# A recurrent layer with experts and grouped attention: the gate's sign products, the last group's end and the reciprocals, reordered

## The chip, the cores and the metric

The kernel runs on 1 core of a Trainium2 chip. The metric is the device time of one execution in microseconds; the number to compare is the median over the runs. The engines are named PE (TensorE, matmul), DVE (VectorE), ACT (ScalarE), POOL (GpSimd) and SP (SyncE, which only issues transfers here). PSUM has eight banks of 128 x 512 fp32, `bank[0]` to `bank[7]`.

## What is computed

Two layers over 2 x 512 tokens of 256 channels. Layer 0 is a chunked selective scan gated by a mixture of 8 experts; it ends at about 315 us and is not touched here. Layer 1, cut to what matters:

```python
q = rope((xn @ Wq.T).reshape(2, 512, 32, 64)); k = rope((xn @ Wk.T).reshape(2, 512, 8, 64)); v = ...
logits = where(causal, q @ k.T / 8, min)          # 4 query heads share one of 8 k/v heads
s = softmax(logits) @ v @ Wo.T
a = sign(layernorm(x) * gamma + beta); signed_w = sign(weight - mean(weight, 1))
g = silu((a @ signed_w.T + bias) * alpha)
x = x + s * g
```

## The kernel before

**Groups and steps.** The 8 k/v heads are 8 groups, worked one after the other. A group has 4 pairs of query heads, a pair 5 steps: 20 steps of one score bank each, some 2.4 us long. `schedule(kind)` (line 76) writes out, as a list of (step, priority, operation, index, index), what happens in each step; every engine walks the same sorted list in `attend` and does its own share of each entry. Within a step the smaller priority comes first. Work that runs over a group's end is "late" and is done in the next group's steps. The kinds are one "first", six "middle", one "last" group, and then "tail", which has only the late work of the last one and the list `ends`.

**The operations** (i is the pair, k the step within it; "b" a batch, "m" a half of the channels):

- **S**: PE computes a bank of scores (L1793 to L1796); DVE takes the negated row maximum (L1031, L1035) into `nmax`.
- **E**: ACT exponentiates the bank with the maximum as bias into `prob`, and accumulates the row sums (L1279).
- **N**, twice a pair, at steps 5i+3 and 5i+5: DVE takes the reciprocal of a head's four row sums (L1040), and POOL multiplies the head's four blocks of `prob` by it (L1471: 128, 256, 384 and 512 columns). DVE first waits on `exp_done` for the exponentials of the step before.
- **T**, 6 steps behind S: PE transposes a bank of `prob` (L1509), ACT copies it rounded to `p_hi` (L1286), DVE subtracts to get `p_lo` (L1044, one input in PSUM). T with k = 0 and k = 2 waits for POOL's products of the pair's first and second head.
- **A**, 2 steps behind T: three products with V on PE (L1513 to L1515). **O** turns a finished pair into `o_hi` (ACT L1293) and `o_lo` (DVE L1048).
- **W**: PE multiplies by Wo for one batch and one half of the channels, DVE adds to `sT` (L1056).
- **Vh, Vl**: the next V rounded to `v_hi` (ACT L1317), and `v_lo` = V - `v_hi` (DVE L1013, both inputs in SBUF, 128 x 256). In the middle and last groups Vl stands in steps 3 and 13, behind N.
- **Q, r, a, h, l**: the next queries: product (PE), rope into `q_mix` (DVE L1001, L1002, one input in PSUM), add (POOL L1480), `q_hi` (ACT L1257), `q_lo` (POOL L1483). **VQ, VO, Kh, Kl**: the same splitting for Wq (POOL L1451), Wo (ACT L1297, POOL L1475) and K (ACT L1264, POOL L1455).
- **Z**: one of the four sign products of the gate (PE L1850, bank 0 or 1), and its Silu on ACT into `g1T` (L1329).

**Order around N.** On every engine an instruction starts only when those ahead of it in its own queue have. On DVE the order within a step is O, S, T, N, Vl, W, r; on POOL N, then a, l, Kl. VO comes ahead of all others of its step, which is step 14; POOL's order there is the four products of step 13, then `wo_lo`, then those of step 15.

**The end.** Before the tail PE waits for the last exponentials (`exp_done`), since Z uses banks 0 and 1. In the tail Z0 to Z3 stand behind A(3,1), A(3,3), A(3,4) and W2. After the list, DVE waits for all W and all four Silus, does the four products `sT * g1T` (L1098), PE transposes them back (L1509, 16 transposes into banks 0 to 3), DVE adds the four banks to `x_tok` (L1102), and SP sends out each half of `x_tok` (L646) when it is complete.

Of the kernel before, what the change touches and what calls it, by code (L numbers as in the profile page):

```python
# [11 lines left out]
P = 128  # L12
BATCH, SEQ, C = 2, 512, 256
T = BATCH * SEQ
NT = T // P
TB = SEQ // P
# [56 lines left out]
def schedule(kind):  # L73

    own = [(14, 0, "VO", 0, 0), (1, 8, "Kh", 1, 0), (2, 6, "Kl", 1, 0)]
    for r in range(PAIRS):
        for k in range(5):
            n = 5 * r + k
            own += [(n, 2, "S", r, k), (n, 4, "E", r, k), (n + LAG, 3, "T", r, k), (n + LAG + TO_V, 5, "A", r, k)]
        for h in range(2):  # L80
            own += [(5 * r + HEADS_AT[h], 5, "N", r, h)]
        own += [(5 * r + 4 + LAG + TO_V + 1, 1, "O", r, 0)]
# [21 lines left out]
    else:  # L104
        ready += [(0, 1, "VQ", 0, 0)] + half(2, 3, 0) + half(3, 13, 0)
    ends = [(4 + 2 * n, 8.6, "Z", n, 0) for n in range(KC * BATCH)]
    lists = {"first": [(own, False), (ready, False)], "middle": [(own, True), (own, False), (ready, False)],
# [56 lines left out]
def layered_kernel(nc, x, params, consts, select, rope, w_in, w_out, w_moe, w_moe_tail, w_qkv, w_o, w_sign, out):  # L164
# [4 lines left out]
    with ctx:  # L169
# [301 lines left out]
        def _(sp):  # L471
# [170 lines left out]
            move_q(KVH - 1, 1)  # L642
            for b in range(BATCH):
                sp.wait_ge(x_ready, NT // 2 + (b + 1) * TB // 2)
                ts = slice(b * TB, (b + 1) * TB)
                sp.dma_start(out.rearrange("(t p) c -> p t c", p=P)[:, ts, :], x_tok[:, ts, :]).then_inc(out_done, 16)  # L646
            sp.wait_ge(out_done, BATCH * 16)


        @block.vector  # L650
        def _(dve):
# [369 lines left out]
            def attend(now, steps):  # L1021
                for late, op, i, k in steps:
# [26 lines left out]
                    elif op == "W":  # L1049
# [3 lines left out]
                        if g == 0:  # L1053
                            vec.tensor_copy(sT[:, m, cs], bank[6 + m][:, :]).then_inc(w_added[m], 1)
                        else:
                            TT(sT[:, m, cs], sT[:, m, cs], bank[6 + m][:, :], ALU.add).then_inc(w_added[m], 1)  # L1056
                    elif op == "r":
                        rope_q(now * 2 + i, k)
# [32 lines left out]
            attend(KVH, schedule("tail"))  # L1091
            for m in range(KC):
                dve.wait_ge(w_added[m], KVH * BATCH)
            for n in range(KC * BATCH):
                s, m = n // KC, n % KC
                cs = slice(s * HALF, (s + 1) * HALF)
                dve.wait_ge(g1_ready, KC * BATCH)
                TT(sT[:, m, cs], sT[:, m, cs], g1T[:, m, cs], ALU.mult).then_inc(sg_ready, 1)  # L1098
            for n in range(NT // 2):
                dve.wait_ge(back_full, n + 1)  # L1100
                xt2 = x_tok[:, 2 * n:2 * n + 2, :]
                TT(xt2, xt2, bank[n][:, :].rearrange("p (t c) -> p t c", c=C), ALU.add).then_inc(x_ready, 1)  # L1102


        @block.scalar
        def _(act):
# [159 lines left out]
            def attend(now, steps):  # L1266
                for late, op, i, k in steps:
# [58 lines left out]
                    elif op == "Z":  # L1326
                        m, s = i // 2, i % 2
                        act.wait_ge(sign_full, i + 1)
# [178 lines left out]
        def _(pe):  # L1507
# [263 lines left out]
            def attend(now, steps, held):  # L1771

                for late, op, i, k in steps:
# [68 lines left out]
                    elif op == "G":  # L1842
                        turn_norm(i, h_ready, bank[6 + i % 2])
                        held[i % 2] = (sign_ready, i + 1)
                    elif op == "Z":
                        m, s = i // 2, i % 2
                        if i > 1:
# [41 lines left out]
            attend(KVH, schedule("tail"), [(w_added[m], (KVH - 1) * BATCH) for m in range(KC)])  # L1889
            for n in range(NT // 2):  # L1890
                pe.wait_ge(sg_ready, KC * (n // (TB // 2) + 1))
                for j in range(2 * KC):
                    t, m = 2 * n + j // KC, j % KC
                    ins = tr(bank[n][:, j * P:(j + 1) * P], sT[:, m, t * P:(t + 1) * P])
                ins.then_inc(back_full, 1)

# [72 lines left out]
```

## Time and profile before

| | us |
|---|---|
| median of 3 runs (767.24 to 769.56) | 767.31 |
| profiled execution: time | 765.41 |
| profiled execution: span | 763.6 |
| PE busy | 712.9 (93%) |
| PE weight load busy | 623.1 (82%) |
| DVE busy | 482.1 (63%) |
| ACT busy | 416.7 (55%) |
| POOL busy | 397.5 (52%) |
| mean granted PE clock | 0.986 |

The profile is of one execution; its span lies inside its time, and the 1.8 us between the two are around the program. Times in the rows are counted from the span's start. The attention groups run from about 336 to 735 us, one group in 48.9 us in the steady part, and the tail from there to 763.6. A row's "idle before" counts from the recorded end of the engine's preceding instruction.

### The profile page before, as it was taken

What the parts mean: (1) busy time and instruction counts of PE and PEld (TensorE: products, weight loads), DVE (VectorE), ACT (ScalarE), POOL (GpSimd) and SP (SyncE); (2) the same over time, 40 slices, a digit from 0 to 9 for tenths busy, and PEclk for the clock granted to TensorE, in tenths of its full rate; (3) what the DMA queues carried; (4) which work ended last, traced back from release to release, by engine and by line L of the source; (5) the groups of instructions that cost most, each with busy time, mean ns of one, the idle gap of its engine ahead of it and who ended that gap; (6) DMA issues with size and microseconds to landing.
All of it is one profiled execution on the core that took longest, in us unless ns stands there. A gap on an engine that the chain in (4) does not pass through costs nothing.

```text
span 763.6 us, 13451 instructions
## 1 busy us (share of the span) xinstructions
PE 712.9 (93%) x4576; PEld 623.1 (82%) x4576; DVE 482.1 (63%) x1030; ACT 416.7 (55%) x1043; POOL 397.5 (52%) x449
## 2 busy tenths in 40 slices
PE   2999999999999999796979999999999999999995
PEld 2887989989989897575768888888888888888883
DVE  7582655334333427866557777777787777777764
ACT  4446244134243233466466677667766777667662
POOL 1412442422332322138487787677867778677460
PEclk9999999999999999899899999999999999999999
DMA  8186877776877835173133322232223322132001
GB/s 292 37 259 191 280 247 233 244 250 191 279 238 239 246 86 138 32 226 84 56 106 82 77 66 60 70 90 64 63 68 78 90 54 66 48 91 57 1 1 56
DMA packets 103828, 98.06 MB, mean 128 GB/s; under 512 B 50576, under 2 KB 74064, under 8 KB 103632
## 3 DMA queue, kind: packets, MB, share of 16 engines
q1 hardware_dynamic: 101648, 91.43, 41.3%
q0 software_dynamic: 2112, 5.77, 2.3%
q8 instruction: 37, 0.61, 0.3%
q14 instruction: 31, 0.25, 0.1%
HBM read 69.24 MB, written 11.14 MB: 105 GB/s over the span
## 4 chain that ended last, share of the span: by engine, by line
PE 64%; DVE 11%; POOL 10%; ACT 7%; issue 4%; SPq 2%; DMA 1%; DVEq 0%; ACTq 0%
PE bank L1653 14%; PE bank L1687 8%; PE bank L1509 7%; PE bank L1513 7%; PE bank L1514 7%; PE bank L1515 7%; POOL prob L1471 5%; ACT prob L1279 3%; PE bank L1793 3%; DVE nmax L1035 2%; PE bank L1794 2%; POOL q_lo L1483 2%; ACT p_hi L1286 2%; DVE o_lo L1048 1%; POOL wq_lo L1451 1%
## 5 line engine op out<-in xcount | busy, mean ns | idle before, releaser
L1471 POOL TENSOR_TENSOR prob<-prob,rinv 128x128 f32<-128x128 f32 (+3 forms) x256 | 177.6, 725 | 103.0 <-DVE rinv L1040 103.0
L1279 ACT ACTIVATE prob<-bank,nmax 128x512 f32<-128x512 f32 (+3 forms) x256 | 133.2, 528 | 48.0 <-DVE nmax L1035 47.7
L1044 DVE TENSOR_TENSOR p_lo<-bank,p_hi 128x512 fp32r<-128x512 f32 x160 | 110.1, 688 | 52.5 <-ACT p_hi L1286 51.6
L1286 ACT ACTIVATE p_hi<-bank 128x512 fp32r<-128x512 f32 x160 | 96.3, 602 | 76.9 <-PE bank L1509 76.8
L1653 PEld LDWEIGHTS bank<-xgT,wm 128*128 128x128 f32 x920 | 108.7, 192 | 4.5 <-issue 2.9
L1653 PE MATMUL bank<-xgT,wm 128*128 128x128 f32 x920 | 111.3, 275 | 0.5 <-ACT xgT L1195 0.5
L1035 DVE TENSOR_REDUCE nmax<-bank 128x1 f32<-128x512 f32 (+2 forms) x192 | 91.2, 503 | 16.3 <-PE bank L1796 15.8
L1509 PE MATMUL bank<-cst,prob 128*128 128x128 f32 x640 | 97.9, 276 | 3.0 <-ACT prob L1279 1.2
L1793 PE MATMUL bank<-kT,qT 128*128 128x512 f32 (+3 forms) x256 | 82.2, 326 | 12.4 <-ACT prob L1279 6.9
L1513 PE MATMUL bank<-p_hi,v_lo 128*128 128x128 f32 (+3 forms) x256 | 92.9, 363 | 0.3 <-DVE p_lo L1044 0.3
L1442 POOL DMA_INDIRECT y_rows<-y_row,to_row x21 | 22.7, 1081 | 118.3 <-DVE y_row L904 92.6
L1515 PE MATMUL bank<-p_hi,v_hi 128*128 128x128 f32 (+3 forms) x256 | 82.3, 322 | 0.0
L1514 PE MATMUL bank<-p_lo,v_hi 128*128 128x128 f32 (+3 forms) x256 | 82.3, 322 | 0.0
L1509 PEld LDWEIGHTS bank<-cst,prob 128*128 128x128 f32 x640 | 73.7, 142 | 6.0 <-POOL prob L1471 3.3
L1794 PE MATMUL bank<-kT,qT 128*128 128x512 f32 (+3 forms) x256 | 74.7, 323 | 0.0
L1793 PEld LDWEIGHTS bank<-kT,qT 128*128 128x128 f32 x256 | 48.4, 189 | 22.5 <-issue 8.4
L1220 ACT ACTIVATE sil<-bank 128x512 f32<-128x512 f32 x23 | 13.7, 597 | 75.9 <-PE bank L1653 75.9
L1687 PE MATMUL bank<-wm,hE 128*128 128x256 f32 x230 | 53.5, 379 | 1.2 <-DVE y_low L909 1.2
L1279 ACT ACTIVATION_READ_ACCUMULATOR prob<-bank,nmax 128x1 f32 x256 | 52.4, 205 | 0.0
L944 DVE TENSOR_TENSOR hE<-sil,bank 128x512 f32<-128x512 f32 x23 | 15.8, 688 | 57.5 <-PE bank L1653 40.6
L1794 PEld LDWEIGHTS bank<-kT,qT 128*128 128x128 f32 x256 | 48.6, 190 | 3.9
L1515 PEld LDWEIGHTS bank<-p_hi,v_hi 128*128 128x128 f32 x256 | 48.4, 189 | 2.7
(307 smaller groups left out, 1534.8 us busy)
## 6 DMA issues: line engine op xcount, KB each, us to landing
wm<-in_w_moe SPq DMA_DIRECT2D x23, 1280.0 KB, 5.8
wm<-in_w_moe SPq DMA_DIRECT2D x23, 640.0 KB, 5.1
qT<-q_hi SPq DMA_DIRECT2D x124, 64.0 KB, 2.0
qT<-q_lo SPq DMA_DIRECT2D x124, 64.0 KB, 2.0
k_exp<-k_rows SPq DMA_DIRECT2D x56, 64.0 KB, 2.0
wtl<-in_w_moe_tail SPq DMA_DIRECT2D x46, 64.0 KB, 5.4
y_rows<-gate SPq DMA_DIRECT2D x1, 2048.0 KB, 13.7
wq_raw<-in_w_qkv SPq DMA_DIRECT2D x32, 64.0 KB, 2.5
```

Source lines behind the costliest of these rows:

```text
L1044: TT(p_lo[:, b_, :], bank[2 + b_ % 2][:, :], p_hi[:, b_, :].bitcast(F32), ALU.subtract).then_inc(plo_done, 1)
L1279: ins = actv(prob[:, i % 2, h, POFF[j]:POFF[j] + (j + 1) * P], bk[:, at:at + (j + 1) * P], ACT.Exp, bias=nmax[:, i % 2, h, j:j + 1], accum ...
L1286: actv(p_hi[:, b_, :], bank[2 + b_ % 2][:, :], ACT.Copy).then_inc(phi_done, 1)
L1471: ins = GT(seg, seg, rinv[:, i % 2, k, j:j + 1].to_broadcast([P, (j + 1) * P]), ALU.mult)
L1509: return nc.tensor.transpose(dst, src, ident)
L1513: mm(dst, w_l, m_h, start=start, stop=False)
L1514: mm(dst, w_h, m_l, start=False, stop=False)
L1515: return mm(dst, w_h, m_h, start=False, stop=stop)
L1653: ins = mm(dst, w(c), xgT[:, u, c, :], start=c == 0, stop=c == KC - 1)
L1687: ins = mm(bank[3][:, 0:C], hE[:, u, i * P:(i + 1) * P], wm[:, s, i, PJ:WM] if i < FULL else ptl[:, s, :], start=i == 0, stop=i == HC - 1)
L1793: mm(dst, qs, kT[:, b, 0, 0:n], start=(h, j, at) == SCORES[k][0], stop=False)
L1794: mm(dst, qs, kT[:, b, 1, 0:n], start=False, stop=False)
```

## The change

Three things are done:

- **N** gets priority 2.6 in place of 5 in all groups. On DVE the reciprocal then stands behind S and ahead of T; Vl, which stood directly behind N, stands behind T.
- In the tail, **Z** n stands in step n: behind the first steps' W, T, A in place of behind the last ones. Z0 and Z1 now make batch 0's gate, Z2 and Z3 batch 1's.
- The closing products, transposes and additions become operations of the tail's list: **M** (DVE product `sT * g1T` for one half of the channels and one batch), **B** (PE, two transposes back), **X** (DVE addition to `x_tok` of one bank). Those of batch 0 stand among the last steps: M(0,0) behind T(3,3), M(1,0) behind T(3,4), B0 ahead of A(3,4), B1 behind it, X0 and X1 behind O3. Those of batch 1 stand behind W2 and W3. The output is sent in three pieces: batch 0, then a quarter, then the last quarter.

```diff
@@ schedule
         for h in range(2):
-            own += [(5 * r + HEADS_AT[h], 5, "N", r, h)]
+            own += [(5 * r + HEADS_AT[h], 2.6, "N", r, h)]
...
-    ends = [(4 + 2 * n, 8.6, "Z", n, 0) for n in range(KC * BATCH)]
+    ends = [(n, 8.6, "Z", n, 0) for n in range(KC * BATCH)]
+    ends += [(4 + m, 9, "M", m, 0) for m in range(KC)] + [(10 + m, 9, "M", m, 1) for m in range(KC)]
+    ends += [(6 + n, 9, "B", n, m) for n in range(2) for m in range(KC)] + [(11 + m, 9.1, "B", n, m) for m in range(KC) for n in (2, 3)]
+    ends += [(8 + n, 9.2, "X", n, 0) for n in range(2)] + [(13, 9.2, "X", n, 0) for n in (2, 3)]
@@ SP
-            for b in range(BATCH):
-                sp.wait_ge(x_ready, NT // 2 + (b + 1) * TB // 2)
-                ts = slice(b * TB, (b + 1) * TB)
+            for lo, hi in ((0, TB), (TB, TB + 2), (TB + 2, NT)):
+                sp.wait_ge(x_ready, NT // 2 + hi // 2)
+                ts = slice(lo, hi)
                 sp.dma_start(out.rearrange("(t p) c -> p t c", p=P)[:, ts, :], x_tok[:, ts, :]).then_inc(out_done, 16)
@@ DVE, attend
+                    elif op == "M":
+                        cs = slice(k * HALF, (k + 1) * HALF)
+                        dve.wait_ge(w_added[i], (KVH - 1) * BATCH + (k + 1))
+                        dve.wait_ge(g1_ready, KC * (k + 1))
+                        TT(sT[:, i, cs], sT[:, i, cs], g1T[:, i, cs], ALU.mult).then_inc(sg_ready, 1)
+                    elif op == "X":
+                        dve.wait_ge(back_full, i + 1)
+                        xt2 = x_tok[:, 2 * i:2 * i + 2, :]
+                        TT(xt2, xt2, bank[i][:, :].rearrange("p (t c) -> p t c", c=C), ALU.add).then_inc(x_ready, 1)
@@ DVE, behind the tail
-            for m in range(KC):
-                dve.wait_ge(w_added[m], KVH * BATCH)
-            for n in range(KC * BATCH):
-                s, m = n // KC, n % KC
-                cs = slice(s * HALF, (s + 1) * HALF)
-                dve.wait_ge(g1_ready, KC * BATCH)
-                TT(sT[:, m, cs], sT[:, m, cs], g1T[:, m, cs], ALU.mult).then_inc(sg_ready, 1)
-            for n in range(NT // 2):
-                dve.wait_ge(back_full, n + 1)
-                xt2 = x_tok[:, 2 * n:2 * n + 2, :]
-                TT(xt2, xt2, bank[n][:, :].rearrange("p (t c) -> p t c", c=C), ALU.add).then_inc(x_ready, 1)
@@ ACT and PE, attend
                     elif op == "Z":
-                        m, s = i // 2, i % 2
+                        m, s = i % 2, i // 2
@@ PE, attend
+                    elif op == "B":
+                        b = i // 2
+                        pe.wait_ge(sg_ready, KC * b + k + 1)
+                        if i < 2:
+                            pe.wait_ge(g1_ready, KC * BATCH)
+                        for t in range(2):
+                            ins = tr(bank[i][:, (t * KC + k) * P:(t * KC + k + 1) * P],
+                                     sT[:, k, (2 * i + t) * P:(2 * i + t + 1) * P])
+                        if k == KC - 1:
+                            ins.then_inc(back_full, 1)
@@ PE, behind the tail
-            for n in range(NT // 2):
-                pe.wait_ge(sg_ready, KC * (n // (TB // 2) + 1))
-                for j in range(2 * KC):
-                    t, m = 2 * n + j // KC, j % KC
-                    ins = tr(bank[n][:, j * P:(j + 1) * P], sT[:, m, t * P:(t + 1) * P])
-                ins.then_inc(back_full, 1)
```

## Rows read from the trace of the kernel before

**Rows 1.** Totals of waits, 330 to 764 us: total us, times, longest.

```profile
POOL prob L1471 <- DVE rinv L1040: 103.0, 48, 6.6
...
PEld bank L1509 <- POOL prob L1471: 3.3, 10, 1.4
```

**Rows 2.** Chain of waits, 632 to 652 us: start, us, what.

```profile
641.39 0.09 DVE rinv L1040
...
641.55 2.76 POOL prob L1471 x4
...
650.81 0.66 PE bank L1509 x4
```

**Rows 3.** Timeline around step 3, group 2: start, us, engine, line, operation [idle before <-releaser].

```profile
458.19 0.17 DVE L1040 RECIPROCAL rinv<-rsum 128x4 f32<-128x4 f32 x1
458.28 0.39 DVE L1013 TENSOR_TENSOR v_lo<-v_exp,v_hi 128x256 fp32r<-128x256 f32 x1
...
458.44 2.84 POOL L1471 TENSOR_TENSOR prob<-prob,rinv 128x128 f32<-128x128 f32 x4 [1.90 <-DVE rinv L1040]
...
458.74 0.76 DVE L1035 TENSOR_REDUCE nmax<-bank 128x1 f32<-128x384 f32 x2
...
459.81 0.69 DVE L1044 TENSOR_TENSOR p_lo<-bank,p_hi 128x512 fp32r<-128x512 f32 x1 [0.31 <-ACT p_hi L1286]
...
461.93 0.69 DVE L1035 TENSOR_REDUCE nmax<-bank 128x1 f32<-128x512 f32 x1 [0.24 <-PE bank L1796]
...
463.01 0.69 DVE L1044 TENSOR_TENSOR p_lo<-bank,p_hi 128x512 fp32r<-128x512 f32 x1 [0.38 <-ACT p_hi L1286]
```

**Rows 4.** Timeline around step 13, group 1.

```profile
434.14 2.85 POOL L1471 TENSOR_TENSOR prob<-prob,rinv 128x128 f32<-128x128 f32 x4 [3.14 <-DVE rinv L1040]
...
434.29 0.75 DVE L1035 TENSOR_REDUCE nmax<-bank 128x1 f32<-128x384 f32 x2
...
435.24 0.69 DVE L1044 TENSOR_TENSOR p_lo<-bank,p_hi 128x512 fp32r<-128x512 f32 x1 [0.20 <-ACT p_hi L1286]
...
436.95 1.28 POOL L1475 TENSOR_TENSOR wo_lo<-wo_raw,wo_hi 128x512 fp32r<-128x512 f32 x1
```

**Rows 5.** Timeline, last group: a score's weight load.

```profile
704.77 0.19 PEld L1793 LDWEIGHTS bank<-kT,qT 128*128 128x128 f32 x1 [0.39 <-ACT prob L1279]
```

**Rows 6.** Timeline, layer 0: a POOL and a DVE product, both on SBUF tiles.

```profile
112.94 1.05 POOL L1398 TENSOR_TENSOR decay_in<-cst,dts 128x512 f32<-128x512 f32 x1
112.97 1.57 DVE L877 TENSOR_TENSOR state<-state,since 128x512 f32<-128x512 f32 x1 [0.92 <-PE bank L1621]
```

**Rows 7.** Timeline, first group, a v_lo of step 7.

```profile
354.05 2.53 POOL L1483 TENSOR_TENSOR q_lo<-q_mix,q_hi 128x512 fp32r<-128x512 f32 x2
...
356.08 2.03 DVE L1013 TENSOR_TENSOR v_lo<-v_all,v_hi 128x256 fp32r<-128x256 f32 x1
...
356.53 1.30 POOL L1460 TENSOR_TENSOR v_all<-v_all 128x512 f32<-128x512 f32 x1
```

**Rows 8.** Timeline of the tail.

```profile
736.02 0.66 PE L1509 MATMUL bank<-cst,prob 128*128 128x128 f32 x4 [1.19 <-ACT prob L1279]
...
744.84 0.60 PE L1850 MATMUL bank<-signT,wsT 128*128 128x512 bf16 x2
...
748.18 0.19 PEld L1513 LDWEIGHTS bank<-p_hi,v_lo 128*128 128x128 f32 x1 [0.83 <-DVE p_lo L1044]
...
750.66 0.47 PE L1513 MATMUL bank<-o_hi,wo_lo 128*128 128x512 f32 x1 [1.05 <-DVE o_lo L1048]
...
752.33 0.69 DVE L1056 TENSOR_TENSOR sT<-sT,bank 128x512 f32<-128x512 f32 x1 [1.82 <-PE bank L1515]
...
754.96 2.50 DVE L1098 TENSOR_TENSOR sT<-sT,xnT 128x512 f32<-128x512 f32 x4
...
757.37 2.47 DVE L1102 TENSOR_TENSOR x_tok<-x_tok,bank 128x512 f32<-128x512 f32 x4
```

**Rows 9.** Transfers, 750 to 764 us: GB/s in 40 slices of 0.35 us.

```profile
GB/s 0 0 0 0 0 47 0 0 0 0 0 0 0 0 0 0 0 0 0 0 0 0 0 0 0 0 0 170 351 345 307 366 337 354 345 345 76 0 0 0
```

More of the change, by code:

```diff
@@ L642, in _ @@
             move_q(KVH - 1, 1)
-            for b in range(BATCH):
-                sp.wait_ge(x_ready, NT // 2 + (b + 1) * TB // 2)
-                ts = slice(b * TB, (b + 1) * TB)
+            for lo, hi in ((0, TB), (TB, TB + 2), (TB + 2, NT)):
+                sp.wait_ge(x_ready, NT // 2 + hi // 2)
+                ts = slice(lo, hi)
                 sp.dma_start(out.rearrange("(t p) c -> p t c", p=P)[:, ts, :], x_tok[:, ts, :]).then_inc(out_done, 16)
-            sp.wait_ge(out_done, BATCH * 16)
+            sp.wait_ge(out_done, 3 * 16)
         @block.vector
@@ L1844, in attend @@
                         held[i % 2] = (sign_ready, i + 1)
+                    elif op == "B":
[8 more added lines that the diff above has]
+                            ins.then_inc(back_full, 1)
                     elif op == "Z":
-                        m, s = i // 2, i % 2
+                        m, s = i % 2, i // 2
                         if i > 1:
```

## The prediction

> **What bounds the kernel now.** The page's shares come first: TensorE works 93% of the span, so in each stage the question is who holds TensorE up. Then the totals of waits from 330 us on: GpSimd sits 103 us idle before the products, waiting for reciprocals, yet TensorE in turn waited for products only 3.3 us, in ten places, 1.4 of it in one [rows 1]. GpSimd's idle time as such is worth nothing; those places are. The chain of waits of a middle group shows one: reciprocal at 641.39, then products, q_lo, wq_lo, the next products, and only then TensorE at 650.81 [rows 2]. GpSimd works through these jobs without a pause, so the start of the first sets the end of the last. Last comes the tail, from 736 us to the end, read as a timeline [rows 8].
>
> **Part 1a, N before T: what it gives.** The vector engine's order S, T, N becomes S, N, T (letters as in the section on the kernel). Its instructions of 0.69 start 0.60 apart, so the N at 458.19 moves to 457.60, and GpSimd starts at 457.84 in place of 458.44 [rows 3]. Does N now wait? It needs the exponentials of the step before. For the 62 reciprocals that have a T ahead I set the end of those exponentials beside the end of S: all but one are done by then (closest 0.06 us); the one is the tail's, which still comes 2.1 us earlier than now. So TensorE's waits for GpSimd go. The 1.4 is a place without a T ahead and stays; the other nine average 0.21 [rows 1], and with the overlap between instructions that each breaks I take 0.26 at the six middle places like 650.81 and 0.2 at two of the last group: 2.0 us. Where T itself waited for p_hi, N falls into that gap and leaves a vector chain on which TensorE later waits: 0.08 apiece, 12 times, 1.0. Together 3.0; bounds 0 (the wait only passes to another engine) and 3.6.
>
> **Part 1b: what it costs.** In steps 3 and 13 of every group but the first, Vl follows. Before: N 458.19, v_lo 458.28, products 458.44: v_lo is ahead of GpSimd [rows 3]. Now T lies between: N 457.60, T 457.68, products 457.84, v_lo 458.28. v_lo reads both its inputs from SBUF and meets GpSimd at work. What that does is in the trace. A vector product of two SBUF tiles that starts at 112.97, 0.03 behind a GpSimd one, takes 1.57 and ends 0.55 after it [rows 6]; vector work of this size takes 0.69 [rows 3]. And a v_lo that starts at 356.08 inside q_lo takes 2.03, not 0.39: it ends at 358.11, 0.28 after GpSimd has finished not q_lo (356.58) but also the job queued behind it (357.83) [rows 7]. GpSimd's jobs overlap by about 0.05, and v_lo did not get in between. The reverse is in every group: with v_lo just ahead, the four products take 2.84 or 2.85 [rows 3, 4], not 2.76 [rows 2]. The reductions, p_lo and the rope products read PSUM, and beside GpSimd keep their 0.69; in the attention loop only v_lo is exposed.
>
> So in step 3 v_lo ends at 457.84 + 2.75 + 0.28 = 460.87 and the reduction behind it starts 0.09 before that, at 460.78 in place of 458.74: 2.04 late. Behind it lie slack places: the idle times at 459.81, 461.93 and 463.01, 0.31 + 0.24 + 0.38 [rows 3], each 0.09 more for the overlap it breaks, and N's 0.08: 1.29. From there the vector work runs without a pause into the chain for which TensorE's scores of step 10 wait. Cost 0.75. In step 13 wo_lo is queued right behind the products [rows 4]: 433.54 + 2.75 + 1.25 + 0.28 = 437.82, reduction at 437.72 in place of 434.29, 3.43 late, less a slack of 0.20 [rows 4], again 0.24 and 0.38, the overlaps and N: 1.17. Cost 2.26. A middle group: 0.75 + 2.26 - 0.26 = 2.75, six of them 16.5. The last group has no rope work and fewer slack places: TensorE's score at 704.77 already stood 0.39 for just these exponentials [rows 5], so the lateness passes on nearly whole, 2.1 and 3.3, less 0.2 each for GpSimd: 5.0. Part 1 costs 21.5 us, the 2.0 of 1a taken off. Queued behind the waiting v_lo are the step's reduction, T and rope; through the reduction the exponentials and TensorE's scores wait for it.
>
> On this the Trainium skill speaks (SBUF — State Buffer, Who interferes with whom): a VectorE instruction with two SBUF inputs contends with a GpSimd one that reads SBUF, and whoever is first has the shared ports for the whole instruction. The 1.57 of [rows 6] agrees. Taken at its word it would free v_lo at the end of one instruction; [rows 7] shows two.
>
> **Part 2, the tail.** The four sign products Z (two 512-column matmuls each, 0.60 for both [rows 8], 0.44 where the next work follows closely) move ahead; their banks are free, since TensorE stood 1.19 for the last exponentials anyway [rows 8]. The table load for Silu moves in front of Z0's activation, where the scalar engine waits in any case. Ahead of the last A there are now two Z more, partly in place of the 0.83 that TensorE stood there [rows 8], and the first batch's products M (0.61 each, a quarter of 2.50 [rows 8]) and transposes B. Played forward from 736.02 with start-to-start times: four Z put the fourth T at 745.3, its p_hi at 746.3 behind Z3's activation, its p_lo at 746.95; M0 0.61 later at 747.56, the last p_lo at 748.17 (was 747.44, 0.74 before the last A), M1 748.77, its transposes 0.74 later at 749.5, and the last A at 749.7 in place of 748.18. TensorE's queue behind that new wait is A, B, W2, W3. From there on the same distances as now: W2 2.5 behind A, its add 1.7 behind W2, so 753.9; then M 754.7, second add 755.3, M 756.1, its transposes 756.8, the last addition to x at 757.9, where before it was the last of four from 757.37, at 759.2 [rows 8]. Two products and two additions have left the end, against the 1.5 lost before A: 1.3 gained. The output: before, both halves moved back to back from 759.5 to 762.9, and the span ended 3.7 behind the last addition (759.88). Now half is out early and 256 KB stand behind the last addition, beside 256 KB issued 0.6 ahead; 1 MB takes 3.0 [rows 9]. Gain 1.1. The third issue on SP costs nothing while it lies beside the second's transfer; else its 0.6. Tail together 2.4; bounds 0.5 (M and B in the way) and 3.3.
>
> **Sum.** The profiled execution has span 763.6 and time 765.41. 763.6 + 21.5 - 2.4 = 782.7, its time 784.5. The median of the runs is 767.31, 1.9 above that execution, and I forecast against it: 767.3 + 19.1 = 786.4.
>
> **The rivals.** *A, the forecast:* v_lo waits until GpSimd pauses. 786.4; 781 to 791 for the sizes of the slack and for a lower clock in places, should TensorE's new idle times bring one (in the tail it kept full clock through idle times of 1 to 2 us). Chance 0.70.
> *B, the other side: v_lo slips in between two products.* It would start 1.2 behind N, the reduction be 0.2 to 0.4 late, and the slack swallows that. Part 1 gives its 3.0, the tail 2.4: 761.9. It turns at a lateness of about 1.2 per v_lo, the slack. For it: each product is an instruction of its own. Against it: [rows 7], though a single case. Chance 0.16. By the Trainium skill's sentence above it would be this one.
> *C: v_lo waits out the four products but slips in before wo_lo.* 1.25 less in each step 13, 8.7 in all: 777.7. Chance 0.10.
> *D: v_lo waits, and slack hides nearly all of it:* 765 to 769. Chance 0.04.
>
> **How the numbers follow.** The likeliest is A, 786.4. Leaving B and D out leaves out 0.2, so the range takes in C and A: 777 to 791; A's own is 781 to 791. Faster than 765.0 (by 0.3%, about what a measurement of this kernel tells from no change): B and a little of D, 0.17; within it 0.04; slower 0.79.
>
> **What would show it.** In A the 14 v_lo take near 2.6 (step 3) and 3.8 us (step 13), not 0.39, and the products 2.75; the reductions of steps 4 and 14 are late, TensorE has new waits for exponentials, and a middle group lasts 51.6 us, not 48.9. In B v_lo stays below 1 us and a group is 48.4. In the tail: last A to last addition 8.2 us (now 11.0), last addition's end to the end of the span 2.6 (now 3.7). I would be wrong if GpSimd gave way inside a run of its work, or if the wait for M1 held up TensorE longer than 1.5 us.

## The result and the profile after

The changed kernel takes 761.01 us in the median of 6 runs (760.19 to 762.42), the kernel before 767.27 (765.38 to 769.56, 6 runs): ratio 0.9926, 95% interval 0.9911 to 0.9941. It is faster, by 6.3 us in the medians and 5.7 by the ratio; the forecast was 786.4, slower by 19. What happened is rival B of the prediction, priced at 761.9: v_lo gets in between two products. The profiled execution has time 760.74 and span 758.9.

The page of the kernel after, part 1, then the totals of waits from 330 us on (us in all, times, longest), which answer to [rows 1]:

```profile
PE 710.7 (94%) x4576; PEld 622.7 (82%) x4576; DVE 485.8 (64%) x1030; ACT 418.1 (55%) x1043; POOL 399.2 (53%) x449
...
POOL prob L1472 <- DVE rinv L1043: 95.7, 44, 6.9
...
PEld bank L1510 <- POOL prob L1472: 1.4, 1, 1.4
```

TensorE's waits for products are gone but for the one place without a T ahead, which the prediction left standing. Next, both v_lo rows of the kernel after by tile (duration in ns: least, median, most; first and last start):

```profile
L1016 DVE TENSOR_TENSOR v_lo<-v_exp,v_hi x14: 835/839/840, 409.1 to 722.1; 128x256 fp32r<-128x256 f32 x14
...
L1016 DVE TENSOR_TENSOR v_lo<-v_all,v_hi x2: 394/585/776, 343.3 to 356.4; 128x256 fp32r<-128x256 f32 x2
```

All 14 that now start beside the products take 0.84 us, not 2.6 and 3.8. The timeline of the kernel after at step 3 of group 2 and, behind the dots, at step 13 of group 1 answers to [rows 3, 4]:

```profile
456.88 0.17 DVE L1043 RECIPROCAL rinv<-rsum 128x4 f32<-128x4 f32 x1
456.96 0.66 DVE L1047 TENSOR_TENSOR p_lo<-bank,p_hi 128x512 fp32r<-128x512 f32 x1
...
457.13 2.94 POOL L1472 TENSOR_TENSOR prob<-prob,rinv 128x128 f32<-128x128 f32 x4 [1.90 <-DVE rinv L1043]
...
457.54 0.84 DVE L1016 TENSOR_TENSOR v_lo<-v_exp,v_hi 128x256 fp32r<-128x256 f32 x1
458.30 0.74 DVE L1038 TENSOR_REDUCE nmax<-bank 128x1 f32<-128x384 f32 x2
...
432.65 0.17 DVE L1043 RECIPROCAL rinv<-rsum 128x4 f32<-128x4 f32 x1
...
432.89 2.94 POOL L1472 TENSOR_TENSOR prob<-prob,rinv 128x128 f32<-128x128 f32 x4 [3.16 <-DVE rinv L1043]
...
433.31 0.84 DVE L1016 TENSOR_TENSOR v_lo<-v_exp,v_hi 128x256 fp32r<-128x256 f32 x1
434.07 0.74 DVE L1038 TENSOR_REDUCE nmax<-bank 128x1 f32<-128x384 f32 x2
...
435.80 1.29 POOL L1476 TENSOR_TENSOR wo_lo<-wo_raw,wo_hi 128x512 fp32r<-128x512 f32 x1
```

The order of starts is the forecast's: N, T, products, v_lo 0.41 us into them. But v_lo ends at 458.38, when the second of the four products is over, and not behind all four (460.07) or behind wo_lo. The reduction starts 1.42 us behind N, where it was 0.55; N itself is 0.60 earlier, so it is late by 0.27. At step 13 the kernel before has

```profile
433.90 0.17 DVE L1040 RECIPROCAL rinv<-rsum 128x4 f32<-128x4 f32 x1
```

and the reduction 0.39 behind it [rows 4]; now it is 1.42 behind again, which makes it late by 0.43. Like steps of consecutive middle groups are 48.47 us apart, against 48.87: 0.40 gained a group.

The first group of the kernel after, in the place of [rows 7]:

```profile
354.32 2.54 POOL L1484 TENSOR_TENSOR q_lo<-q_mix,q_hi 128x512 fp32r<-128x512 f32 x2
...
356.37 0.78 DVE L1016 TENSOR_TENSOR v_lo<-v_all,v_hi 128x256 fp32r<-128x256 f32 x1
...
356.82 1.48 POOL L1461 TENSOR_TENSOR v_all<-v_all 128x512 f32<-128x512 f32 x1
```

The instructions are those of [rows 7] (the job that GpSimd runs into the tile v_all is a rope addition for K) and v_lo is issued as far ahead of q_lo's end, yet now it goes in front of that job, which is called v_all below. The row on which the forecast rested has come out the other way.

The last group and the tail of the kernel after, a timeline with the idle time and its releaser in brackets, which answers to [rows 8]:

```profile
702.49 0.19 PEld L1794 LDWEIGHTS bank<-kT,qT 128*128 128x128 f32 x1 [0.82 <-ACT prob L1280]
702.49 0.44 PE L1794 MATMUL bank<-kT,qT 128*128 128x384 f32 x1 [0.38 <-ACT prob L1280]
...
733.76 0.66 PE L1510 MATMUL bank<-cst,prob 128*128 128x128 f32 x4 [1.51 <-ACT prob L1280]
...
747.22 0.44 PE L1510 MATMUL bank<-cst,sT 128*128 128x128 f32 x2 [0.44 <-DVE sT L1064]
747.42 0.36 PE L1514 MATMUL bank<-p_hi,v_lo 128*128 128x256 f32 x1
...
749.88 0.47 PE L1514 MATMUL bank<-o_hi,wo_lo 128*128 128x512 f32 x1 [1.07 <-DVE o_lo L1051]
...
751.54 0.69 DVE L1059 TENSOR_TENSOR sT<-sT,bank 128x512 f32<-128x512 f32 x1 [0.63 <-PE bank L1516]
...
754.89 1.29 DVE L1068 TENSOR_TENSOR x_tok<-x_tok,bank 128x512 f32<-128x512 f32 x2 [0.53 <-PE bank L1510]
```

and its transfers, 745 to 759 us in 40 slices, which answer to [rows 9], with the output's pieces (KB each, median us from issue to landing):

```profile
GB/s 0 0 0 0 0 0 0 0 0 47 0 0 0 0 0 0 0 0 0 99 357 342 354 322 24 0 0 0 0 0 0 0 20 334 342 345 342 114 0 0
...
out_x<-x_tok SPq DMA_DIRECT2D x1, 512.0 KB, 2.9
out_x<-x_tok SPq DMA_DIRECT2D x2, 256.0 KB, 2.2
```

In the last group TensorE has a new wait of 0.38 for exponentials. It is at the place of [rows 5], where only the weight load had waited, 0.39; that load now waits 0.82. The output leaves in two blocks of 512 KB: batch 0 while W is still being worked on, and both quarters together, behind the end of the last addition at 756.18. From TensorE's start on the tail to the end of the span it is 758.9 - 733.76 = 25.1 us; before it was 763.6 - 736.02 = 27.6.

### The profile page after: what moved, and what is told of

The parts are those of the page before. It is cut to its first block, busy times and chain, and to the rows that moved or that the text cites. A ratio compares the mean times of both kernels' runs of the same rounds, so it can differ in the third digit from the quotient of the medians.

```text
span 758.9 us, 13459 instructions
## 1 busy us (share of the span) xinstructions
PE 710.7 (94%) x4576; PEld 622.7 (82%) x4576; DVE 485.8 (64%) x1030; ACT 418.1 (55%) x1043; POOL 399.2 (53%) x449
## 4 chain that ended last, share of the span: by engine, by line
PE 69%; DVE 11%; ACT 8%; issue 5%; POOL 2%; SPq 2%; DMA 1%; DVEq 0%; ACTq 0%; POOLq 0%
PE bank L1654 14%; PE bank L1514 8%; PE bank L1515 8%; PE bank L1516 8%; PE bank L1510 8%; PE bank L1688 8%; ACT prob L1280 4%; PE bank L1794 3%; PE bank L1795 3%; DVE nmax L1038 3%; ACT p_hi L1287 2%; DVE o_lo L1051 2%; PE bank L1797 1%; ACT o_hi L1294 1%; DVE q_mix L1004 1%
## 5 line engine op out<-in xcount | busy, mean ns | idle before, releaser
L1794 PEld LDWEIGHTS bank<-kT,qT 128*128 128x128 f32 x256 | 48.4, 189 | 22.8 <-issue 8.5
L1221 ACT ACTIVATE sil<-bank 128x512 f32<-128x512 f32 x23 | 13.7, 596 | 75.9 <-PE bank L1654 45.4
L1516 PEld LDWEIGHTS bank<-p_hi,v_hi 128*128 128x128 f32 x256 | 48.4, 189 | 2.7
```

Source lines behind the costliest of these rows:

```text
L1516: return mm(dst, w_h, m_h, start=False, stop=stop)
L1794: mm(dst, qs, kT[:, b, 0, 0:n], start=(h, j, at) == SCORES[k][0], stop=False)
```

## The experiments

Rival B is called theory S (a waiting vector instruction gets the ports at the end of one GpSimd instruction), the forecast theory K (GpSimd keeps them until it pauses). One caution on reading: up to the first v_lo all kernels have the same instructions, and yet it starts anywhere between 342.7 and 346.7 us. So single profiles are compared by the distance from the first v_lo to the end of the span: 420.5 in the kernel before, 415.6 after. Repeats show how far that is good: 420.4 for the kernel before once more, and 415.2 and 415.5 for two kernels (e13 and e14) that were to carry an extra instruction in the middle groups but, by a condition that never held there, executed the instructions of the changed kernel again. By the distance the change is worth 4.8 to 5.3 us, less than the 5.7 to 6.3 of the timed runs; where the rest lies these profiles do not show.

**Each part alone.** The tail alone is the changed kernel with

```diff
-            own += [(5 * r + HEADS_AT[h], 2.6, "N", r, h)]
+            own += [(5 * r + HEADS_AT[h], 5, "N", r, h)]
```

> The tail part alone: N stands where it stood before, behind the group's scores; the last steps are the changed ones. On record: the tail gives 2.4 us and has nothing to do with the v_lo subtraction, so the time is 767.3 - 2.4 = 764.9 us (the profile of the changed kernel has 25.14 us from TensorE's start on the last steps to the end of the span, against 27.56: the same 2.4). TensorE's start on the tail should stay at about 736.0 and its end at about 761.1. If the tail's gain came only together with the earlier reciprocals (rival), the time stays within 0.5 us of 767.3. The first group's v_lo, which stands beside q_lo in this kernel as in the one before: theory K (GpSimd keeps the shared ports until it pauses) gives 2.0 us again; theory S (a waiting VectorE instruction gets them at the end of one GpSimd instruction) gives 0.8; a near-tie at the boundary gives either.

and the reciprocals alone are the kernel before with 2.6 in place of 5.

> The reciprocals alone: N directly behind the maximum, the last steps the old ones. On record as the forecast: slower by 21.5 - 3.0 = 18.5 us, 785.8 (v_lo of 2.6 and 3.8 us in 14 groups). The profile of the changed kernel already speaks against that: its v_lo beside GpSimd's products takes 0.84 us and a middle group is shorter by 0.40 us. So now: 6 middle groups... 11 distances between the v_lo subtractions of the last products shown by that profile give 2.3 us by the start of the tail, and the time is 767.3 - 2.3 = 765.0 us (range 764.3 to 765.4). If the two parts were not independent (rival: the changed tail is what lets the groups run closer), it is within 0.5 us of 767.3 and e1_tail_only carries all 6.3 us.

Measured against 766.07 us for the kernel before on the same chip: the tail alone 763.44, ratio 0.9958 (0.9945 to 0.9971); the reciprocals alone 763.38, ratio 0.9962 (0.9948 to 0.9975). Split at TensorE's start on the tail:

| kernel | first v_lo to tail | tail to end | sum |
|---|---|---|---|
| before | 392.9 | 27.6 | 420.5 |
| changed | 390.5 | 25.1 | 415.6 |
| tail alone | 393.4 | 25.2 | 418.5 |
| reciprocals alone | 390.6 | 27.5 | 418.2 |

The parts are independent: each shortens its own stretch and leaves the other, within the error of such a comparison. The 18.5 us of loss on record for the reciprocals are not there. The tail alone has 0.4 to 0.5 us more ahead of the tail than the kernel before, of which 0.3 arise before the first middle group is through; that is the size of such a comparison's error.

**v_lo ahead of the products.** In the middle and last groups v_lo goes directly behind N:

```diff
-        own += [(n + 2, 8, "Vh", b, 0), (n + 3, 8, "Vl", b, 0)]
+        own += [(n + 2, 8, "Vh", b, 0), (n + 3, 8 if kind == "first" else 2.7, "Vl", b, 0)]
```

> The changed kernel with v_lo of the middle and last groups put directly behind N, so that it starts before GpSimd's products do and meets none of them. Theory S, with the collision charged to what stands behind it: v_lo 0.39 us again instead of 0.84, products 2.84 instead of 2.94, and the vector chain behind it (nmax) starts 0.45 us earlier; since the group's length is set by TensorE, of that only what TensorE waited for comes back: in the last group 0.2 to 0.5 us, in the middle groups nothing or up to 0.1 each. Time 760.3 us, range 759.3 to 761.0. Theory that the 0.84 us are free (all hidden): within 0.2 us of 761.0. Rival: v_lo ahead of the products makes p_lo and TensorE's T later by 0.39 us in each of 14 groups: up to 761.0 + 5.5 = 766.5 us.

759.50 us, ratio 0.9916 (0.9902 to 0.9930); the interval overlaps the changed kernel's, so the gain is read from the profiles. v_lo takes 0.39 in all 14. First v_lo to tail 389.5, so 1.0 us less than in the changed kernel, and the whole distance 414.7. Middle groups stay at 48.47: the 0.45 us is hidden there. What comes back is at the ends, above all in the last group, whose wait of 0.38 at 702.49 (and its twin at 724.67) is gone. So the collision costs 0.8 us by the whole distance and 1.0 by the stretch ahead of the tail, of which the two waits are 0.75; expected was 0.7 (760.3 us for 761.0).

**v_lo inside the last product.** One step later (`n + 4`, priority 5.5):

> The changed kernel with v_lo of the middle and last groups one step later, so that it is issued while GpSimd runs the last of its four products. In the second step 4 of a pair of chunks GpSimd has its half of wo_lo queued directly behind; in the other nothing is queued behind. Theory K (the ports stay with GpSimd while it has queued work): v_lo ends only behind wo_lo where that is queued, so 0.4 + what is left of the product + 1.3, about 2 us or more, and below 1.1 us where nothing is queued. Theory S (the waiting instruction gets in at the end of the GpSimd instruction that is running): below 1.1 us in all 14, and wo_lo's GpSimd half starts no earlier than v_lo's end or shares with it. Near-tie theory (what decides is how closely the two requests fall together): both values occur among the like groups. Time within 1 us of 761.0 by S, up to 5 us over it by K.

The timeline of this kernel at its second v_lo of a group, wo_lo queued:

```profile
434.62 0.74 DVE L1016 TENSOR_TENSOR v_lo<-v_exp,v_hi 128x256 fp32r<-128x256 f32 x1
...
433.26 1.83 POOL L1472 TENSOR_TENSOR prob<-prob,rinv 128x384 f32<-128x384 f32 x2
435.04 1.48 POOL L1476 TENSOR_TENSOR wo_lo<-wo_raw,wo_hi 128x512 fp32r<-128x512 f32 x1
```

Thirteen of 14 take 0.73 to 0.74, seven of them with wo_lo queued; the 14th (700.65) was issued just as the last product began and takes 1.26, that product and 0.28. v_lo passes in front of wo_lo, which takes 1.48 in place of 1.29. Time 759.33. Beside the products and wo_lo theory K is refuted: queued work did not keep the ports in any of these cases.

**The path behind v_lo.** Was the forecast's other half right, that two late v_lo of a group would cost 3.0 us? Here the vector engine is held behind v_lo for as long as the forecast had it wait:

```diff
+                        if k == 4 and i in (0, 2) and not (isinstance(now, int) and now == 0):
+                            for _ in range(3 if i == 0 else 5):
+                                vec.tensor_reduce(out=hold[:, i + _:i + _ + 1], in_=bk[:, :], op=ALU.max, axis=AX.X, negate=True)
```

> The changed kernel, and behind v_lo, ahead of the reduction of its next step, the vector engine is held with reductions of a full bank into a scratch column that nobody reads: three in the step behind the first v_lo of a group, five in that behind the second, in every group but the first. They read PSUM alone and start 0.60 apart, so that the reduction behind v_lo comes 1.8 and 3.0 us later, with the 0.2 to 0.4 that it is late already about the 2.04 and 3.43 us of the forecast. This holds up everything of the forecast but the ports. If the path part of the forecast was right (slack 1.3 and 1.2 us, the rest passes on), the time is near the forecast, 761.0 + 24.5 = 785.5 us, a pair of v_lo 0.75 + 2.26 us dearer and a distance between like steps of two groups near 51.6 us. If slack hides nearly all (rival D), 761 to 765. If the slack is smaller than read, up to 761.0 + 14 x 2.4 = 794.6.

and with `range(1)` in place of `range(3 if i == 0 else 5)`:

> The same with a single reduction in each place, 0.60 us. By the forecast's slack (rival B turns at a lateness of about 1.2 us for a v_lo) the lateness is 0.2 to 0.4 + 0.6 and still inside it: middle groups as in the changed kernel, within 0.05 us of 48.47, and only the last group, with fewer places of slack, 0.3 to 0.9 us longer; time 761.0 to 762.0. If there is no slack, every held 0.60 us passes on: 14 x 0.6 = 8.4 us, 769.4.

The held kernel takes 791.71 us. Its timeline, step 13 of group 1:

```profile
436.30 0.84 DVE L1017 TENSOR_TENSOR v_lo<-v_exp,v_hi 128x256 fp32r<-128x256 f32 x1
437.06 3.06 DVE L1035 TENSOR_REDUCE hold<-bank 128x1 f32<-128x512 f32 x5
440.06 0.73 DVE L1042 TENSOR_REDUCE nmax<-bank 128x1 f32<-128x384 f32 x2
...
441.90 0.44 PE L1798 MATMUL bank<-kT,qT 128*128 128x384 f32 x1 [1.08 <-ACT prob L1284]
```

The reductions behind the held places come 3.22 and 4.42 us behind N; counted like the 0.27 and 0.43 above they are 2.07 and 3.43 late, just what the forecast had (2.04 and 3.43). A middle group lasts 51.99 us, 3.52 more than in the changed kernel (forecast: 3.01 more, 51.6 us), so the slack of the two places is 5.50 - 3.52 = 1.98 together, where 2.46 was read. Six such groups make 21.1, the last group and what follows 8.1 (forecast 5.4). Of the 8.1 only 4.8 are the eight added reductions of 0.60. The rest goes together with a lower clock of TensorE, by the kernel's windows from 722.8 us on (busy time and instructions of each engine, granted clock, DMA share, GB/s):

```profile
722.80:727.30 4.50, 2.09 (x12) 1.25 (x11) 4.50 (x10) 1.90 (x8) 2.56 (x4) 1.00 0.05 13
727.30:730.70 3.40, 3.40 (x14) 3.40 (x15) 1.97 (x6) 2.08 (x6) 2.75 (x4) 0.50 0.02 5
730.70:754.60 23.90, 20.27 (x133) 17.40 (x133) 18.23 (x36) 14.13 (x44) 9.95 (x14) 1.00 0.00 0
754.60:758.00 3.40, 3.40 (x18) 3.40 (x16) 1.97 (x4) 2.02 (x7) 2.42 (x4) 0.50 0.02 5
```

TensorE stood idle 2.16 us up to 727.24 and 3.35 up to 754.01, and from 727.3 and from 754.6 on the granted clock is 0.50 for 3.4 us, the lower of its two levels (1.2 GHz); in the changed kernel it is 1.00 all through this stretch. Two like products start 0.46 us apart at 727.24 and 0.28 at 754.01, where the clock was still full; by these the 6.8 us at half clock cost some 2.7 us, an estimate, of the 3.3 that are left to explain. That the clock does it is argued, not tested.

With a single reduction the middle groups last 48.46, nothing more. In the last group TensorE's two waits for exponentials are 0.97 each in place of 0.38, 1.2 us in all, and the whole distance is 417.0, time 762.06: the reduction passes on whole there. So the middle groups' slack is real, about a fifth smaller than read, and beyond it lateness passes on; the last group has none. With that lateness the kernel is slower (791.71) than the forecast's 786.4 and than the 785.5 expected of this run.

**The kernel before once more.**

> The kernel before once more, for one reading: the v_lo of 2.03 us at 356.08, on which the forecast rests. Of the kernels so far that have the same instructions around this place it took 2.03 us in five and 0.77 in five. If what GpSimd has queued decided it (theory K), it takes 2.03 us here again; if the boundary is a near-tie, it takes either, and 0.77 in the kernel before itself would settle that the change is not what turned it. The distance from the first v_lo to the end of the span, 420.5 us in the trace of before, should repeat within 0.3.

2.02 us again at 356.09, distance 420.4. The kernel before alone would not have shown that this boundary can fall either way. All 20 profiles together do: one kernel, the next, issues v_lo elsewhere; in the other 19 it comes through in 8 (0.77 to 0.92 us) and not in 11 (2.02 to 2.03). Kernels with the same instructions up to there are on both sides: the changed kernel (0.78) and the two that executed its instructions again (2.03 and 2.02), or the one that differs from it only in the output's pieces (2.03).

**That v_lo inside the first q_lo.**

```diff
-        own += [(n + 2, 8, "Vh", b, 0), (n + 3, 8, "Vl", b, 0)]
+        own += [(n + 2, 8, "Vh", b, 0), (n + 3, 2.7 if kind == "first" and b else 8, "Vl", b, 0)]
```

> The changed kernel with one instruction moved: the first group's second v_lo stands ahead of p_lo instead of behind it, so that it is issued at about 354.9, inside the first of the two q_lo instructions (it ends at about 355.6), with the second q_lo and then v_all queued on GpSimd. In the place behind p_lo this v_lo came through at the end of the second q_lo (0.77 us) in five of thirteen kernels and only behind v_all (2.03 us) in eight, always issued 0.49 us ahead of the boundary. If the kind of instruction that GpSimd has next decides (v_all keeps the ports, a like instruction does not), it comes through at the first q_lo's end, 0.9 to 1.0 us, as 98 of 98 did between two products. If q_lo itself keeps them, 2.3 us (behind the second q_lo) or 3.5 us (behind v_all too). The time stays within 0.5 us of 761.0: the vector engine stood 0.81 us idle here.

Timeline of this kernel:

```profile
354.18 3.53 DVE L1016 TENSOR_TENSOR v_lo<-v_all,v_hi 128x256 fp32r<-128x256 f32 x1
...
353.63 2.55 POOL L1484 TENSOR_TENSOR q_lo<-q_mix,q_hi 128x512 fp32r<-128x512 f32 x2
356.11 1.31 POOL L1461 TENSOR_TENSOR v_all<-v_all 128x512 f32<-128x512 f32 x1
```

It waits behind three GpSimd instructions, two boundaries, and ends 0.29 behind the last, as theory K has it, in this place. The time is 759.85, so it costs nothing here. Its other 14 v_lo take 0.84.

**The same kind of instruction beside other GpSimd work.** An extra subtraction of v_lo's size, into a tile nobody reads, in the six middle groups:

```diff
+                    if (op, i, k) in [('S', 3, 4), ('N', 3, 1)] and 0 < now < KVH - 1:
+                        TT(side[:, [('S', 3, 4), ('N', 3, 1)].index((op, i, k)), :], x_tok[:, 0, :], turns[:, 0, 0:C], ALU.subtract)
```

> The changed kernel with an extra vector subtraction of v_lo's kind (128x256, both inputs in SBUF, into a tile that nobody reads) at two places of each of the six middle groups: S, issued inside the third of GpSimd's four products (the fourth is queued), and N, issued inside the first of two q_lo (the second, and a weight's low part behind it, are queued). At S a product is running and it should come through at its end, 0.7 to 1.1 us, six of six. At N: if what is running decides (a product lets the waiting instruction in, a subtraction of two whole tiles keeps the ports), it waits behind q_lo, q_lo and the weight's part, 3 us or more, in most of them; if the place in the first group was special, 0.7 to 1.1 us as at S. The kernel's time rises by what slack does not hide, 0 to 12 us.

The second kernel has it at `('T', 2, 4)` and `('T', 0, 4)`, the third at `('S', 0, 1)` and `('S', 3, 2)`.

> The same extra subtraction, in the six middle groups, at two other places: T24, inside the second q_lo with a weight's low part (another subtraction of two tiles) queued, and T04, inside the second q_lo with a product queued. If what is running decides, both wait past the boundary in most cases. If what is queued decides (a product gives way, a subtraction does not), T04 comes through at q_lo's end, about 1.0 to 1.4 us, and T24 does not, 2 us or more. Near-tie: both mixed, as the fifteen v_lo at the boundary between q_lo and v_all in the first group (five through, ten not).

> The same extra subtraction at two more places of the six middle groups: S01, inside a weight's low part (wq_lo) with a product queued, and S32, inside the first of two rope additions (q_mix, in place) with the second queued. If what is running decides, both wait past the boundary: S01 behind all four products, about 3 us or more, or into a gap between two of them, about 1.3; S32 behind both additions, about 1.7 us. If what is queued decides, S01 comes through at wq_lo's end, 0.8 to 1.0 us, and S32 does not.

Timelines: of the first kernel, a place N; of the second, a place T24:

```profile
449.66 1.06 DVE L1080 TENSOR_TENSOR side<-x_tok,turns 128x256 fp32r<-128x256 f32 x1
...
449.15 2.73 POOL L1487 TENSOR_TENSOR q_lo<-q_mix,q_hi 128x512 fp32r<-128x512 f32 x2
```

```profile
400.83 0.90 DVE L1080 TENSOR_TENSOR side<-x_tok,turns 128x256 fp32r<-128x256 f32 x1
...
398.90 2.54 POOL L1487 TENSOR_TENSOR q_lo<-q_mix,q_hi 128x512 fp32r<-128x512 f32 x2
401.40 1.47 POOL L1455 TENSOR_TENSOR wq_lo<-wq_raw,wq_hi 128x512 fp32r<-128x512 f32 x1
```

At N it ends at 450.72 while the pair of q_lo runs to 451.88: it went in between the two, and the pair takes 2.73 for 2.54. At T24 it goes in front of wq_lo, which takes 1.47 for 1.29. All 36 come through at the first end: 0.89 to 1.06 at N and S, 0.90 at T24, 1.41 at T04, 0.88 at S01, 0.41 at S32, where the first rope addition was nearly over. The times are 762.53, 760.53 and 761.79. So neither the kind of work that runs nor the kind that is queued decides.

**Place or form.** One packed subtraction where the kernel above had v_lo, and twelve in the middle groups that read v_all as that v_lo does:

```diff
+                    if (op, i, k) == ("S", 1, 2) and now == 0:
+                        TT(side[:, 0, :], x_tok[:, 0, :], turns[:, 0, 0:C], ALU.subtract)
+                    if (op, i, k) in [("N", 3, 1), ("T", 0, 4)] and 0 < now < KVH - 1:
+                        TT(side[:, i // 3, :].rearrange("p (t c) -> p t c", c=HD), v_all[:, TB:NT, 0:HD],
+                           turns[:, 0, 0:C].rearrange("p (t c) -> p t c", c=HD), ALU.subtract)
```

> 36 of 36 extra subtractions in the middle groups came through at the end of the GpSimd instruction that was running, whatever ran or was queued. What is left is the place in the first group, or the form of v_lo there: it reads 4 x 64 columns out of v_all, rows 512 apart, and not v_exp, packed. This kernel separates the two. One extra subtraction with packed inputs stands in the first group where e12_first_vlo had v_lo (inside the first q_lo), and two a middle group, twelve in all, read v_all as v_lo does there (inside the first q_lo, and inside the second with products queued). Place: the packed one waits 3.5 us behind both q_lo and v_all, or 2.3, and the twelve come through in 0.9 to 1.5 us. Form: the packed one comes through at the first q_lo's end, about 1.0 us, and most of the twelve wait past a boundary, 2 us or more (inside the first q_lo 3.5). Both values among the twelve would be a near-tie by the form. The first group's own v_lo behind it takes 0.77 or 2.03 us again.

```profile
354.29 1.02 DVE L1080 TENSOR_TENSOR side<-x_tok,turns 128x256 fp32r<-128x256 f32 x1
...
355.83 0.92 DVE L1017 TENSOR_TENSOR v_lo<-v_all,v_hi 128x256 fp32r<-128x256 f32 x1
```

All 13 come through, and so does the first group's own v_lo, issued 0.64 us ahead of q_lo's end instead of 0.49. Neither the place alone nor the form alone does it. What is left is both together, or a chance that only this v_lo has; that stays open.

**The tail's own edits.** TensorE's wait for the last exponentials in front of the first Z instead of the first T:

> The changed kernel with TensorE's wait for the last exponentials put in front of its first Z job instead of in front of the tail's first transpose. The profile of the changed kernel has TensorE idle for 1.51 us at 733.76 with that wait, and the first thing of the tail that reads a probability of the last exponentials comes only later; the transposes ahead of it need the products of GpSimd that are done. Theory (the wait stands too early, the idle time is the tail's own loss): the tail, from the last groups' scores to the end of the span, is shorter by about 1.3 us, and the idle row of 1.5 us goes. Rival (what stands behind it, GpSimd's last products or the vector chain, is late as well): under 0.3 us, with a row of about the same length at the next instruction. The first group's v_lo again takes 2.0 or 0.77 us, whichever way the boundary behind q_lo falls.

M and B of the first batch one step later (`5` for `4 + m`, `7` for `6 + n`):

> The changed kernel with the first batch's closing multiplications (M of batch 0 and the transposes B behind them) put one step later, so that they stand behind the last T and A of the tail and not between them. In the profile of the changed kernel TensorE waits 0.44 us for M at 747.22 and two B stand ahead of the last A at 747.42. Theory (the interleaving costs what stands in front of the last A): last A at 746.4, 1.0 us earlier, and the span 0.5 to 1.0 us shorter. Rival (the closing work of batch 0 then meets that of batch 1 on the vector engine and TensorE, and the gain is lost): span within 0.3 us of the changed kernel's, or up to 0.7 us longer.

Output in two pieces:

> The changed kernel with its output stored in two pieces of 512 KB, one a batch, instead of 512 KB and two of 256 KB. In the changed kernel the last X ends 2.7 us ahead of the span's end, and a piece of 256 KB takes 2.2 us from issue to landing, one of 512 KB 2.9. Theory (the last piece's size sets the stretch behind the last X): that stretch is 3.3 to 3.5 us and the span 0.6 to 0.75 us longer; with the old kernel's 3.7 us that is the 1.1 us of the output part less what the pieces' shape does. Rival (only the earlier first batch matters, not how the rest is cut): within 0.2 us.

By distance, against the 415.2 to 415.6 of the changed kernel (415.5 is taken): 413.8, 414.6 and 416.1; times 758.60, 760.91 and 762.45, one run each. The early wait cost 1.7 us by this and 1.6 from the last group's first v_lo on (57.5 for 59.1), about TensorE's idle row of 1.51; the first T of the tail now runs at 731.62 without a wait. M and B between the last T and A cost 0.9; the stretch from TensorE's start on the tail to the end is 24.2 us for 25.1. The cut of the last half gives 0.6 of the output's 1.1.

**All three edits together**, with v_lo behind N:

> All three together: v_lo directly behind N as in e3_vlo_behind_n, TensorE's wait at Z, the first batch's closing work behind the last A. If the three are independent: 1.0 (e3's gain by the profiles) + 1.3 + 0.5 to 1.0 = 2.8 to 3.3 us under the changed kernel, 757.9 us against 767.3 of the kernel before, ratio 0.987 to 0.988. Rival (the tail has one chain behind all of them, the vector engine's, and the gains overlap): 1.0 to 1.8 us under the changed kernel, 759.2 to 760.0, ratio 0.989 to 0.991.

756.83 us (757.9 was expected), ratio 0.9880 (0.9864 to 0.9897), below the changed kernel's interval. Distance 412.3, 3.2 under the changed kernel, against 0.8 + 1.7 + 0.9 = 3.4 for the parts: within the error they add. This is the fastest kernel here.

## Why the prediction was wrong, by its own steps

*What bounds the kernel* held. The few places where TensorE waited for GpSimd were worth something, its 103 us of idle time nothing.

*Part 1a, the gain*: 3.0 forecast. With v_lo out of the way (v_lo directly behind N) the stretch ahead of the tail is 389.5 for 392.9: 3.4. Per middle group 0.40, where 0.26 + 2 x 0.08 = 0.42 was taken. Right there; the ends of the stretch gave 1.0 where 0.5 had been taken, and a few tenths of that are the comparison's error.

*Part 1b, the cost*, is the step that failed, and in it one sentence: that v_lo, 0.4 us into the products, waits until GpSimd pauses. Everything ahead of it was right (the distances between the starts of N, T, products and v_lo, to 0.02 us), and what stood behind it was near: held up as long as the forecast had it, the vector engine makes a middle group 51.99 us long, where 51.6 was announced (the slack was read 0.5 too large, and the last group, at 8.1 for 5.4, 2.7 too cheap). But the reduction behind v_lo was late by 0.27 and 0.43 and not by 2.04 and 3.43, inside a slack of about 1, and the collision cost 0.8 to 1.0 us in place of 23.5 (21.5 and the 2.0 that were taken off it). The evidence for the sentence was one row [rows 7], against four products that are four instructions; the trace of before has no second vector instruction with two SBUF inputs that waited inside a run of GpSimd instructions. The row was no misreading: v_lo did wait there behind a queued job, it does so in 11 of 19 kernels, and once behind two. But beside the products v_lo came through at the end of the one that was running in 196 of 196 cases, and in 14 of 14 in the last product. A single case told what can happen, not what happens; 0.70 on it and 0.16 on rival B was too much weight for one row.

The Trainium skill (SBUF — State Buffer, Who interferes with whom) gives the shared ports to whoever is first "for the whole instruction". The prediction set that sentence aside for the one row. The runs side with the page: 0.84 us in 14 of 14 here. The row it does not explain is v_lo in the first group.

*Part 2, the tail*: 2.4 forecast, 27.6 - 25.1 = 2.5 measured, and by its steps: last A 13.7 us behind the start (749.7 on record, 747.42 - 733.76 = 13.7 here), last A to last addition 8.1 (8.2), last addition's end to the span's end 2.7 (2.6). Right. The output's gain is 1.0 where 1.1 was taken. And there was more to have: the wait at the tail's first T was read, as cover for the Z products, and not questioned.

*Rival B* said 761.9: 3.0 + 2.4. The kernel has 2.4 + 2.5 by the profiles, the first being 3.4 less the 1.0 of v_lo's collision, most of it in the last group, which has no slack at that place. B's mechanism is the one that the rows show: v_lo below 1 us, the reduction 0.2 to 0.4 late, a middle group of 48.4 us (0.84, 0.27 and 0.43, 48.47). *C* and *D* did not happen: v_lo does not wait out the four products, and by the held kernel slack does not hide a long wait.

*The range* reached from A to C and left out B because B's chance was set below 0.2 on one row. It should have held it.

## What to carry to other kernels

A vector subtraction with two SBUF inputs that is put beside a run of GpSimd instructions ended, outside one place, 0.28 us behind the end of the one that was running. So what it loses depends on how much of that one is left (0.41 us where it was nearly over, 1.41 where it had just begun), and short GpSimd instructions make better company than long ones. At that one place it waited for two or three in some kernels, so look at each place in the trace. When a price far out of the ordinary rests on a single row and the trace has no second case, run a small experiment that makes more cases, or leave the other outcome a chance that keeps it inside the range. And a wait that the code places ahead of a stage is worth as much as its idle row if what it guards is used only later.

## What the runs showed of the hardware that was not expected

Beside GpSimd a waiting vector subtraction of 128x256 came through at the end of the instruction in the way in 259 of 259 cases outside one place (196 v_lo in the second product of 14 kernels, 14 in the last product, 49 extra subtractions beside q_lo, wq_lo, rope additions and products). It ended 0.28 us behind that instruction, and GpSimd's next took 0.19 us longer (wo_lo 1.48 for 1.29). At that one place, the first group's second v_lo, it waited on behind queued work in 11 of 19 kernels, and in a 20th, issued 1.5 us earlier beside the same jobs, behind two boundaries. The 19 divide although the instructions around it are the same in all but one and start within some hundredths of a microsecond at the same distances. What turns it is not known. Neither the kind of GpSimd work running or queued, nor the place alone, nor the stride of the source alone does.
